# Second pair of tokens' router: scores read before the third low half, weights and copy after it

## What is computed

```python
gate_probs = softmax(xf @ gate_W.T, axis=-1)          # 8 experts
weights, sel = top_k(gate_probs, 2)
weights = weights / sum(weights)
w_dense = zeros((T, 8)).at[arange(T)[:, None], sel].add(weights)
h = einsum('td,erd->ter', xf, A)                      # 8 experts of rank 8
h = h * (w_dense[:, :, None] * 2.0)
out = xf @ W_base.T + einsum('ter,eor->to', h, B)
x = layernorm(x + out)
```

## Time and profile before

| | us |
|---|---|
| median of 3 runs | 1959.69 |
| lowest and highest of them | 1957.73, 1960.36 |
| the profiled execution | 1960.41 |
| its span, first to last instruction | 1958.6 |
| TensorE busy in it | 1783.3 (91%) |
| VectorE busy | 1362.4 (70%) |
| ScalarE busy | 792.3 (40%) |

### The profile page before, as it was taken

One profiled execution on the slowest core, in us unless ns is written; L12 is line 12 of the kernel. 1 busy time (PEld: TensorE's weight loads), 2 busy tenths in 40 slices (PEclk: granted clock), 3 DMA queues, 4 the chain that ended last, 5 costly groups with the idle time before them and its releaser, 6 DMA issues. The chain is left out here.

```text
span 1958.6 us, 27039 instructions
## 1 busy us (share of the span) xinstructions
PE 1783.3 (91%) x10210; PEld 952.3 (49%) x10210; DVE 1362.4 (70%) x2607; ACT 792.3 (40%) x939; POOL 171.4 (9%) x362
## 2 busy tenths in 40 slices
PE   3899999999944969999999999998899999999997
PEld 2666666666621434445444445443344444444443
DVE  3888888888859866777666777689655565465553
ACT  5788888888745212222222212133222222122211
POOL 1212121212100000000000000000010010001000
PEclk8999999999976979999999999999999999999999
DMA  8799999999768499999999999955989988988883
GB/s 280 188 292 267 282 257 296 263 289 252 229 197 241 124 233 250 267 251 235 259 258 252 248 231 232 223 167 161 283 249 257 272 235 256 258 259 228 262 251 118
DMA packets 565595, 472.70 MB, mean 241 GB/s; under 512 B 498448, under 2 KB 502544, under 8 KB 544656
## 3 DMA queue, kind: packets, MB, share of 16 engines
q1 hardware_dynamic: 565456, 470.87, 87.7%
HBM read 237.51 MB, written 109.58 MB: 177 GB/s over the span
## 5 line engine op out<-in xcount | busy, mean ns | idle before, releaser
L1585 PE MATMUL bank_f<-w_hi_f,a_cols_f 128*128 128x512 f16 x3584 | 1091.9, 382 | 79.0 <-DMA a_cols_f<-rows_f 58.7
L1585 PE MATMUL bank_f<-w_lo_f,a_cols_f 128*128 128x512 f16 x1792 | 684.4, 382 | 0.0
L1585 PEld LDWEIGHTS bank_f<-w_hi_f,a_cols_f 128*128 128x128 f16 x3584 | 352.5, 98 | 509.3 <-DVE w_lo_f L1312 40.1
L1164 ACT ACTIVATE rows_f<-xn_f 128x1024 f16<-128x1024 f32 x78 | 82.4, 1057 | 497.7 <-DMA xn_f<-x_scratch 339.5
L1585 PEld LDWEIGHTS bank_f<-w_lo_f,a_cols_f 128*128 128x128 f16 x1792 | 176.2, 98 | 204.5 <-issue 4.0
L1343 DVE SCALAR_TENSOR_TENSOR y_f<-bank_f,w_iscale_f,y_f 128x512 f32<-128x512 f32 x192 | 134.6, 743 | 169.2 <-PE bank_f L1585 169.1
L656 PE MATMUL ps_s_fast<-k_both_fast,q_hi_fast 128*128 128x256 f16 x1024 | 171.2, 275 | 8.0 <-DMA k_both_fast<-v_lo_fast 7.0
L1343 DVE SCALAR_TENSOR_TENSOR y_f<-bank_f,w_iscale,y_f 128x512 f32<-128x512 f32 x192 | 134.9, 744 | 45.3 <-PE bank_f L1585 37.3
L1304 DVE TENSOR_TENSOR rows_f<-xn_f,rows_f 128x1024 f16<-128x1024 f32 x78 | 94.4, 1210 | 92.3 <-ACT rows_f L1164 92.3
L1304 DVE TENSOR_TENSOR rows_f<-sums_f,rows_f 128x1024 f16<-128x1024 f32 x63 | 76.9, 1221 | 112.5 <-ACT rows_f L1164 112.4
L1164 ACT ACTIVATE rows_f<-sums_f 128x1024 f16<-128x1024 f32 x63 | 66.3, 1053 | 199.3 <-DMA a_cols_f<-rows_f 196.9
(11 more groups left out here) (215 smaller groups left out, 2288.4 us busy)
## 6 DMA issues: line engine op xcount, KB each, us to landing
xbuf_fast<-x SPq DMA_DIRECT2D x32, 1024.0 KB, 7.9
x_scratch<-x2buf_fast SPq DMA_DIRECT2D x32, 1024.0 KB, 5.5
y_f<-x_scratch SPq DMA_DIRECT2D x32, 1024.0 KB, 8.0
xn_f<-x_scratch SPq DMA_DIRECT2D x62, 512.0 KB, 4.8
kept_scratch<-a_cols_f SPq DMA_DIRECT2D x45, 512.0 KB, 3.4
xn<-x_scratch SPq DMA_DIRECT2D x45, 512.0 KB, 6.7
a_cols_f<-kept_scratch SPq DMA_DIRECT2D x45, 512.0 KB, 9.0
cbuf<-ctx_in SPq DMA_DIRECT2D x16, 1024.0 KB, 5.5
```

The lines of the kernel that those rows point to most:

```text
L1164: nc.scalar.activation(rows[g % 2][:, 0], source(i), ACT.Copy).then_inc(a_hi, 1)
L1585: ins = nc.tensor.matmul(bank[i][:], a_cols[:, i, part + kk, :], ww[:, W_SLOT[i], kk, :], start=(kk == 0 and part == 0 and ww is w_hi), st ...
```

## The change

In slot 1 alone, the router's steps are written in other places. On VectorE `router_scores` goes from behind `low_rows(2, 3)` to ahead of `low_rows(2, 2)`, and `router_weights` from behind `combine(2, 5)` to behind `combine(2, 3)`. On ScalarE `router_exp` goes from behind `high_rows(2, 4)` to behind `high_rows(2, 2)`, and `copy_h` from behind `high_rows(2, 6)` to behind `high_rows(2, 4)`. No instruction is added or taken away. TensorE's and SyncE's orders stay as they are.

```diff
@@ ScalarE @@
                     high_rows(s + 1, 2)
+                    if s == 1:
+                        router_exp(s)
                     high_rows(s + 1, 3)
                     if 1 < s < LAST:
                         copy_h(s)
                     high_rows(s + 1, 4)
                     if s == 1:
-                        router_exp(s)
+                        copy_h(s)
                     high_rows(s + 1, 5)
                     high_rows(s + 1, 6)
-                    if s == 1:
-                        copy_h(s)
@@ VectorE @@
                     update(s, 0, 1)
+                    if s == 1:
+                        router_scores(s)
                     low_rows(s + 1, 2)
                     combine(s + 1, 3)
+                    if s == 1:
+                        router_weights(s)
                     update(s, 2, 3)
                     combine(s + 1, 4)
                     low_rows(s + 1, 3)
-                    if s == 1:
-                        router_scores(s)
-                    else:
+                    if s != 1:
                         update(s, 4, 5)
                     low_rows(s + 1, 4)
                     combine(s + 1, 5)
                     if s == 1:
-                        router_weights(s)
                         update(s, 4, 5)
```

## The result

The change takes **1962.76 us** (median, 1959.65 to 1965.74), the kernel before, run beside it, 1959.78 us (1956.75 to 1964.38). The ratio is 1.0015, with a 95% interval from 1.0008 to 1.0022. The forecast was 1963.0 and no measurable change. The interval excludes 1: the kernel is slower, by 1.6 to 4.3 us. That is still no change in the prediction's sense, which took less than 3.9 us for one. The profiled execution of the change took 1963.30 us with a span of 1961.5, that of before 1960.41 with 1958.6.

What follows compares the result with a forecast made beforehand. TensorE, busy 91% of the span, was taken to bound the kernel, through slot 2's start and clock. Slot 2 1.3 us later plus 2.0 for the clock made 3.3: from 1959.69 to 1963.0 us, range 1957.0 to 1966.0.

Steps and rivals of the forecast that it cites:

- price of the cold start: TensorE at slot 2: starting at half clock behind new waits costs 1.7 to 2.3 us, taken as 2.0.
- slot 2's shift and the clock, together: Slot 2's start: 1.3 us later behind update 12, plus 2.0 us for the cold clock, 3.3 us on the path.
- Scores at no cost: VectorE ahead of low_rows(2, 2): the moved scores, 2.04 us, fit in an idle gap of 2.83 us, so nothing is lost.
- the 2.83 us gap: VectorE idle from about 706.1 to 708.93, waiting for ScalarE; the 2.04 us of scores were to fit there.
- Weights and copy sooner, and not kept: TensorE in slot 1: transposes 7.9 us and matmuls with B 8.2 us sooner, the gain lost to a wait for VectorE.
- The landing, 7.8 us after the issue: SyncE's turn(2, 4): issued at 722.7, lands at 730.5 instead of 726.3, bounds 727.0 to 731.8.
- Rival C: turn(2, 4) lands later, 9.1 us from issue; slot 2 2.6 us later, with the clock 4.6 us, 1964.3; chance 0.18.
- Ring order: SyncE's queue: descriptors taken in ring order give a landing of turn(2, 4) at 730.5; completing ahead of earlier ones, 727.0.
- rival B: turn(2, 4) lands sooner, 4.3 us from issue, at 727.0; slot 2 at 732.7, time 1957.5 to 1959.5; chance 0.14.
- The clock: TensorE idles from about 726 to 730.5 and 731.3 to 736.2, so slot 2 starts at half clock, costing 2.0 us.
- Whatever slot 1 saves or loses is carried on: From slot 2 on: following slots are bound by TensorE, so slot 1's shift, 3.3 us, reaches the total time.

Runs made afterwards that it cites:

- scores alone: Kernel before with only router_scores and router_exp moved as in the change, weights and copy left in place: 1960.30 us, ratio 1.0002.
- updates ahead: The change, plus updates 8 to 13 of slot 1 moved ahead of low_rows(2, 6): 1959.90 us, ratio 0.9994 to the kernel before.
- best version: Kernel before with scores and exponentials moved, copy behind high_rows(2, 5), updates 8 to 13 ahead of low_rows(2, 6), weights left: 1956.67 us, again 1956.11.
- copy alone: Kernel before with only ScalarE's copy moved, from behind high_rows(2, 6) to behind high_rows(2, 5): 1958.87 us, ratio 0.9990.
- turn ahead: The change, plus turn(2, 4) issued on SyncE ahead of the two loads in slot 1: 1960.62 us, ratio 1.0002 to the kernel before.
- both: The change, plus updates 8 to 13 ahead of low_rows(2, 6) and turn(2, 4) ahead of the loads: 1958.62 us, ratio 0.9991.
- all updates first: The change with turn(2, 4) ahead of the loads, plus updates 4 to 13 straight behind combine(2, 5): 1959.13 us, ratio 0.9992.
- filler in the change: The change, plus 180 unread small matmuls on TensorE, 90 ahead of pair 2's last scores and 90 behind: 1960.07 us, ratio 0.9997.
- filler in the best version: The best version, plus 240 unread small matmuls on TensorE ahead of slot 1's transposes: 1959.44 us, ratio 0.9998; again 1957.88, ratio 0.9985.

## Why the prediction was right

Its steps, counted from `low_rows(2, 2)`; the forecast's times are those of the prediction less 708.93, the measured ones those of the rows above less 710.02:

| step, us from D | forecast | after |
|---|---|---|
| transposes start | 6.7 | 6.66 |
| first matmul with B | 10.8 | 10.68 |
| `low_rows(2, 3)` starts | 8.95 | 8.97 |
| `turn(2, 3)` issued | 10.2 | 10.21 |
| `turn(2, 4)` issued | 13.8 | 13.76 |
| `turn(2, 4)` lands | 21.6 | 21.55 |
| `low_rows(2, 6)` starts | 22.7 | 22.68 |
| slot 2 starts | 27.3 | 27.35 |
| price of the cold start | 2.0 | 1.93 |
| **slot 2's shift and the clock, together** | **3.3** | **3.28** |

- **Scores at no cost: right.** VectorE still waits 0.66 us for ScalarE behind them: of the 2.83 us gap, 2.17 are used. Moving the scores alone made no difference that is clear of noise either.
- **Weights and copy sooner, and not kept: right.** TensorE's four waits together are 16.81 us, where before had two of 15.98.
- **The landing, 7.8 us after the issue: right in this execution and the next** (7.85), and in part luck: the reason given, the same transfer behind the same loads, does not fix it. It took 8.7 us with the updates ahead and in the best version, and 8.9 with the copy alone. Rival C, from 8.4 us on, was nearer than its chance of 0.18 says; in the change itself it didn't occur in two executions.
- **Ring order.** The Trainium skill ("DMA: Bandwidth & Descriptors", "Queues, rings and completion order") lets a later descriptor complete ahead of an earlier one. The runs agree with what it says of order and show no case of the exception: in the 11 traces with the loads issued first, the transposition took 7.8 to 10.5 us and landed 1.9 to 3.3 us behind the 1 MB load. Issued ahead of the loads (turn ahead, both, all updates first), it landed 4.7 to 5.2 us after its issue, at 727.8 to 728.3. So the time of rival B, 4.3 us from issue, was near what the transfer takes without the loads, and the loads did stand between.
- **The clock: right.** The cold start costs 1.93 us, shown by the filler; in the other kernels that start slot 2 cold it is 1.5 to 2.7. The prediction had left open when TensorE would be done with B and three groups of scores, 16.3 to 18.5 us from D by the clock. The clock rose at 724.2, and it was done 16.6 us from D. The records have the full clock until about 731; it fell again in the second pair of waits. The Trainium skill ("TensorE: Matmul & The Clock Gate", "HAM oscillation") describes bursts between waits that start cold each time. The runs agree: where all long waits lie ahead of the copy and TensorE then works through with 1.5 us of idling at most (before, scores alone, copy alone, the best version, all updates first), slot 2 starts full; where it idles 3.9 to 9.1 us behind the matmuls with B (the change, updates ahead, turn ahead, both), slot 2 starts at half.
- **"Whatever slot 1 saves or loses is carried on": right for the change, not in general.** 3.28 us at slot 2 have become 2.98 us between the medians, and 3.9 on another chip. With filler in the change 2.84 us became nothing, with all updates first a gain of 5.27 became 1.6, and with filler in the best version a gain of 4.40 became 0.4.

What it didn't see is that the long wait for the copy in the kernel before was no price of the router at all, but of the queue: the earlier trace rows shows the copy right behind `high_rows(2, 6)`, which had waited for the DMA. The prediction used that row for the landing only. Moving the copy by one place is worth about two us (0.2 to 3.9 by the interval); moving the weights with it, which pushes VectorE's low halves and through them SyncE, takes more than that away.

## What to carry to other kernels

Work moved forward on a shared engine delays all that it is moved past: follow each of these to the DMA that it triggers, and from the landing back to the engine that the first one waits for. Several short waits can cost more than one long one, since each may end at half clock; count TensorE's first us behind each wait. And where an engine waits for a step, look first at what this step was queued behind: to take it out from behind a DMA wait may be all there is to win.

## What the runs showed of the hardware

- **One transposing DMA behind the same two loads took 7.8 to 10.5 us from issue to landing, in two parts that vary by themselves.** The first is the 1 MB load ahead of it. It took 6.4 to 6.5 us in most traces, 7.5 in copy alone, and 8.3 and 7.3 in the two traces of the best version with filler, where 3.3 and 2.8 us of the filler ran beside the loads. The second is the time from this load's landing to that of the transposition: 1.9 us in before, the change (twice), scores alone and copy alone; 2.7 to 2.8 in updates ahead, the best version (twice) and filler in the best (twice); 3.3 in filler in the change. So in the best version the filler is all that differs, and what came later with it were the loads (the 512 KB one too, 6.1 and 5.1 us instead of 4.7), not the transposition behind them. Since copy alone has a late load without any filler, the cause is not shown. Nor is that of the second part; the kernels with 2.7 us and more have the updates moved ahead, or filler beside the transposition.
- **240 small matmuls that ended 2.04 us too early did not keep the clock.** They are 80 columns wide and ran 8.76 us without a gap at the full clock; behind 2.04 us of idling, the transposes and 0.69 us more, the matmuls with B were at half.
- **The same matmuls with B and scores stay at half clock for different times.** Counted from the first matmul with B it was 3.5 us in the change, 4.6 in before, and 5.9 in scores alone and the best version.
- **The same kernel reaches the same row up to 2 us apart** (708.73 and 710.71) in two executions whose stretches after it agree within 0.1 us up to slot 2's transposes (43.04 and 42.94).
